# Row normalisations of a two-layer attention and expert kernel computed inside the output stages

## The reference

```
x = x + xattn0(LN(x), ctx, mask)              # 16 heads of 16, then @ Wo.T
s = LN(x)
s1 = LN(s + selfattn(s) @ Wo + bo) * ln1_g + ln1_b
expert = floor(s1 @ router_w + router_b) mod 4    # top-1 expert of each row
x = x + (LN(s1 + expert_ffn(s1)) * ln2_g + ln2_b)
x = x + xattn1(LN(x), ctx, side bias) @ Wo.T + bo
z = LN(x)                                     # top-2 of 16 experts, capacity 320
x = x + experts(z) + mean of 2 shared experts(z)
```

## Time and profile before

| | |
|---|---|
| time, median of 3 runs | 1940.11 us (1938.03 to 1944.42) |
| profiled execution | 1940.5 us |
| its span, first to last instruction | 1938.7 us |
| TensorE busy | 1603.3 us, 83% |
| VectorE busy | 1117.1 us, 58% |
| ScalarE busy | 789.6 us, 41% |
| GpSimd busy | 466.5 us, 24% |

### The profile page before, as it was taken

One profiled execution on the slowest core, in us unless ns is written; L12 is line 12 of the kernel. 1 busy time (PEld: TensorE's weight loads), 2 busy tenths in 40 slices (PEclk: granted clock), 3 DMA queues, 4 the chain that ended last, 5 costly groups with the idle time before them and its releaser, 6 DMA issues. The chain is left out here.

```text
span 1938.7 us, 24242 instructions
## 1 busy us (share of the span) xinstructions
PE 1603.3 (83%) x8256; PEld 1036.7 (53%) x8256; DVE 1117.1 (58%) x2686; ACT 789.6 (41%) x1239; POOL 466.5 (24%) x245
## 2 busy tenths in 40 slices
PE   6799999888999994199717389899868999899993
PEld 3466666554444433199714256556554556566672
DVE  6699999475576747222287488888663441122224
ACT  2388888321455561022103477777612122111110
POOL 0000000020000001311100699999522134111111
PEclk9799999996799997599959699999978999899997
DMA  7533332033222204455335798887342001644424
GB/s 265 199 96 99 98 99 77 24 143 99 55 67 67 77 23 147 160 177 196 122 115 225 256 313 296 284 297 277 133 192 70 1 25 63 209 140 152 153 70 143
DMA packets 136800, 276.56 MB, mean 143 GB/s; under 512 B 23792, under 2 KB 65904, under 8 KB 127088
## 3 DMA queue, kind: packets, MB, share of 16 engines
q1 hardware_dynamic: 129312, 258.98, 40.1%
q0 software_dynamic: 5264, 14.06, 2.1%
q10 hardware_dynamic: 2112, 2.10, 0.3%
HBM read 215.36 MB, written 59.69 MB: 142 GB/s over the span
## 5 line engine op out<-in xcount | busy, mean ns | idle before, releaser
L667 DVE CUSTOM_DVE_ANT_0 X<-pS,M 128x512 f32<-128x512 f32 x512 | 340.2, 689 | 77.2 <-POOL M L593 50.5
L607 PE MATMUL pS<-k,q 65*128 65x512 f32 (+1 forms) x512 | 255.5, 502 | 84.4 <-DVE mx L667 50.1
L593 POOL TENSOR_TENSOR M<-C,M 128x2048 f32<-128x2048 f32 x64 | 290.5, 4588 | 132.5 <-DMA M<-in_fside_Bx16xSxS 132.4
L616 PE MATMUL pT<-ident,X 128*128 128x128 f32 x2048 | 308.3, 274 | 0.3 <-ACT PT L703 0.3
L616 PEld LDWEIGHTS pT<-ident,X 128*128 128x128 f32 x2048 | 256.1, 141 | 40.4 <-issue 3.8
L848 DVE TENSOR_REDUCE nm<-pS 128x1 fp32r<-128x512 f32 x256 | 167.9, 687 | 86.3 <-PE pS L790 74.7
L607 PEld LDWEIGHTS pS<-k,q 65*128 65x128 f32 (+1 forms) x512 | 98.7, 193 | 209.1 <-DVE mx L667 122.5
L500 PE MATMUL pO<-PT,V 128*17 128x512 f32 x1536 | 207.1, 615 | 1.0 <-ACT OT L875 1.0
L695 ACT ACTIVATE X<-X,nm 128x512 f32<-128x512 f32 x256 | 164.0, 712 | 34.6 <-DVE nm L673 34.6
L695 ACT ACTIVATE X<-X,mx 128x512 f32<-128x512 f32 x256 | 164.7, 715 | 21.0 <-DVE mx L667 21.0
L680 DVE COPY PT<-pT 128x1024 f32<-128x1024 f32 x128 | 156.1, 1220 | 6.4 <-PE pT L616 6.4
(11 more groups left out here) (263 smaller groups left out, 2155.8 us busy)
## 6 DMA issues: line engine op xcount, KB each, us to landing
M<-in_fside_Bx16xSxS SPq DMA_DIRECT2D x64, 1024.0 KB, 7.1
w<-in_L_ffn_ew SPq DMA_DIRECT2D x48, 512.0 KB, 4.3
w<-in_L_ffn_W SPq DMA_DIRECT2D x23, 1024.0 KB, 5.4
q<-q_stacks SPq DMA_DIRECT2D x192, 64.0 KB, 3.1
k<-k_stacks SPq DMA_DIRECT2D x128, 64.0 KB, 2.9
M<-mask SPq DMA_DIRECT2D x16, 512.0 KB, 3.6
xs<-top_in SPq DMA_DIRECT2D x51, 128.5 KB, 5.0
k_stacks<-hi SPq DMA_DIRECT2D x24, 256.0 KB, 2.1
```

What stands on the lines that cost most here:

```text
L593: eng.tensor_tensor(M[:, slot], C[:, b % 2], M[:, slot], ALU.subtract).then_inc(s_m, 1)
L607: eng.matmul(pS[:, qt % 2, :], of, by, start=True, stop=True).then_inc(s_s, 1)
L616: ins = eng.transpose(pT[:, kt, qt * P:(qt + 1) * P], X[:, t % 3, qt, kt * P:(kt + 1) * P], self.ident[:])
L667: eng.tensor_tensor_reduce(X[:, i % 3, qt, :], pS[:, qt % 2, :], M[:, slot, qt, :], 2.0 if mask is None else 1.0, HIGHEST if mask is None ...
```

## The change

The normalisations of projection 1, of `route_top1` and of `route_and_share` are taken out of these stages and done by VectorE and ScalarE in the output stage ahead, batch by batch: statistics of a row tile right behind its add, variance and square root per batch, and the scaling of a batch behind the second add of the next. The normalised rows are written over the rows of O that TensorE has already transposed (tile Z, or xx for the router). The weights wo, bo, the projection weights of projection 1 and ln1's rows are fetched in the middle of the attention ahead; those of projections 0 and 2 stay where they were. The normalisations in projections 0 and 2 and in `combine_top1` stay.

```diff
-        self.zeros = self.sb("zeros", [P, S])
+        self.zeros = self.sb("zeros", [P, D])
+        self.Z = self.sb("Z", [P, NT, D + 1])
...
-    def norm_and_transpose(self, block, ctx, bank, banks, src, nat, featT, before=None):
-
-
-        s_ch, s_mv, s_rs, s_z, s_tr, s_ev = (self.sem(n, ctx) for n in ("s_ch", "s_mv", "s_rs", "s_z", "s_tr", "s_ev"))
-        rs = self.normalise(block, s_ch, s_mv, s_rs, s_z, nat, src, ctx, before=before)
+    def turn_rows(self, block, ctx, bank, banks, src, nat, featT, before=None, normal=False):
+
+
+        s_tr, s_ev = (self.sem(n, ctx) for n in ("s_tr", "s_ev"))
+        if not normal:
+            s_ch, s_mv, s_rs, s_z = (self.sem(n, ctx) for n in ("s_ch", "s_mv", "s_rs", "s_z"))
+            rs = self.normalise(block, s_ch, s_mv, s_rs, s_z, nat, src, ctx, before=before)
+
+            @block.scalar
+            def _(eng):
+                self.deviations(eng, s_mv, s_rs, rs)
 
         def tensor(eng, tenant_gone=None):
             for b in range(B):
-                eng.wait_ge(s_z, b + 1)
+                if not normal:
+                    eng.wait_ge(s_z, b + 1)
...
+    def load_weights(self, eng, wq, wk, wv, bq, bk, bv):
+
+        self.s_w = self.sem("s_w")
+        for w, of in zip(self.W, (wq, wk, wv)):
+            eng.dma_start(w[:], of.rearrange("(k p) n -> p k n", p=P)).then_inc(self.s_w, 16)
+        if bq is not None:
+            eng.dma_start(self.bias[:, 0, :], bq).then_inc(self.s_w, 16)
+            eng.dma_start(self.bias[:, 1, :], bk).then_inc(self.s_w, 16)
+            eng.dma_start(self.bvr[:], bv.partition_broadcast(P)).then_inc(self.s_w, 16)
+
+    def load_out(self, eng, wo, bo):
+
+        self.s_wo = self.sem("s_wo")
+        eng.dma_start(self.wo[:], wo.rearrange("(k p) n -> p k n", p=P)).then_inc(self.s_wo, 16)
+        if bo is not None:
+            eng.dma_start(self.bo[:], bo.partition_broadcast(P)).then_inc(self.s_wo, 16)
+
+
+    def project(self, src, nat, qT, kvT, context, q_scale, QS, KS, biased=True, fetch=None, normal=False, mask=None, common=None, first=False, ring=None):
...
-                    for w, of in zip(W, (wq, wk, wv)):
-                        eng.dma_start(w[:], of.rearrange("(k p) n -> p k n", p=P)).then_inc(s_w, 16)
-                    if n_bias:
-                        eng.dma_start(bias[:, 0, :], bq).then_inc(s_w, 16)
-                        eng.dma_start(bias[:, 1, :], bk).then_inc(s_w, 16)
-                        eng.dma_start(bvr[:], bv.partition_broadcast(P)).then_inc(s_w, 16)
+                    if fetch is not None:
+                        fetch(eng)
...
                     for i in range(NBH):
+                        if i == NBH // 2:
+                            fetch(eng)
...
                     for pair in range(NBH // 2):
+                        if pair == NBH // 4:
+                            fetch(eng)
...
-                @block.sync
-                def _(eng):
-                    eng.dma_start(w[:], wo.rearrange("(k p) n -> p k n", p=P)).then_inc(s_w, 16)
-                    if bo is not None:
-                        eng.dma_start(brow[:], bo.partition_broadcast(P)).then_inc(s_w, 16)
...
                 def _(eng):
-                    for n in range(B * KD):
-                        b, k = divmod(n, KD)
-                        eng.wait_ge(s_tr, n + 1)
-                        need(eng, s_y, (b - 1) * ST)
-                        eng.copy(OT[:, b % 2, k, :], bank[:, n % 4, :]).then_inc(s_ev, 1)
+                    def deviations(b):
+                        eng.wait_ge(s_var, b + 1)
+                        rows = slice(b * ST, (b + 1) * ST)
+                        eng.activation(rs[:, rows], rs[:, rows], ACT.Sqrt).then_inc(s_dev, 1)
+
+                    for b in range(B):
+                        for k in range(KD):
+                            n = b * KD + k
+                            eng.wait_ge(s_tr, n + 1)
+                            need(eng, s_y, (b - 1) * ST)
+                            eng.copy(OT[:, b % 2, k, :], bank[:, n % 4, :]).then_inc(s_ev, 1)
+                        if b >= 2:
+                            deviations(b - 2)
+                    deviations(B - 2)
+                    deviations(B - 1)
 
                 @block.vector
                 def _(eng):
-                    if bo is not None:
-                        eng.wait_ge(s_w, 32)
+                    if biased:
+                        eng.wait_ge(self.s_wo, 32)
                         for b in range(B):
                             rows = slice(b * ST, (b + 1) * ST)
                             eng.tensor_tensor(dst[:, rows, :], base[:, rows, :], brow[:].unsqueeze(1).to_broadcast([P, ST, D]),
                                               ALU.add).then_inc(s_b, 1)
-                        eng.wait_ge(s_b, B)
-                    src = base if bo is None else dst
-                    for n in range(NT):
-                        eng.wait_ge(s_y, n + 1)
-                        eng.tensor_tensor(dst[:, n, :], src[:, n, :], py[:, n % 4, 0:D], ALU.add).then_inc(s_a, 1)
-
-
-    def route_top1(self, src, xx, gain, shift, slot, tile_expert, XS):
+                    src = dst if biased else base
+
+                    def stats(n):
+                        eng.wait_ge(s_a, n + 1)
+                        eng.bn_stats(st[:, n, :], dst[:, n, :]).then_inc(s_st, 1)
+
+                    def scale(b):
+                        rows = range(b * ST, (b + 1) * ST)
+                        eng.wait_ge(s_dev, b + 1)
+                        eng.reciprocal(rs[:, b * ST:(b + 1) * ST], rs[:, b * ST:(b + 1) * ST]).then_inc(s_rs, 1)
+                        eng.wait_ge(s_rs, b + 1)
+                        eng.wait_ge(s_tr, (b + 1) * KD)
+                        if affine is None:
+                            for n in rows:
+                                eng.tensor_scalar(z[:, n, :], dst[:, n, :], mv[:, n, 0:1], rs[:, n:n + 1], ALU.subtract, ALU.mult)
+                            return
+                        gain, shift, s_affine = affine
+                        if b == 0:
+                            eng.wait_ge(s_affine, 32)
+                        for n in rows:
+                            eng.scalar_tensor_tensor(out=z[:, n, :], in0=dst[:, n, :], scalar=mv[:, n, 0:1], in1=gain[:],
+                                                     op0=ALU.subtract, op1=ALU.mult).then_inc(s_g, 1)
+                        for n in rows:
+                            eng.wait_ge(s_g, n + 1)
+                            eng.scalar_tensor_tensor(out=z[:, n, :], in0=z[:, n, :], scalar=rs[:, n:n + 1], in1=shift[:],
+                                                     op0=ALU.mult, op1=ALU.add)
+
+                    for b in range(B):
+                        for j in range(ST):
+                            n = b * ST + j
+                            if biased and j == 0:
+                                eng.wait_ge(s_b, b + 1)
+                            eng.wait_ge(s_y, n + 1)
+                            eng.tensor_tensor(dst[:, n, :], src[:, n, :], py[:, n % 4, 0:D], ALU.add).then_inc(s_a, 1)
+                            if j > 0:
+                                stats(n - 1)
+                            if j == 1 and b > 0:
+                                scale(b - 1)
+                        stats((b + 1) * ST - 1)
+                        eng.wait_ge(s_st, (b + 1) * ST)
+                        for n in range(b * ST, (b + 1) * ST):
+                            eng.bn_aggr(mv[:, n, :], st[:, n, :]).then_inc(s_ag, 1)
+                        eng.wait_ge(s_ag, (b + 1) * ST)
+                        eng.tensor_scalar(rs[:, b * ST:(b + 1) * ST], mv[:, b * ST:(b + 1) * ST, 1], EPS, None, ALU.add).then_inc(s_var, 1)
+                    scale(B - 1)
...
-                rs = self.normalise(block, s_ch, s_mv, s_rs, s_z, xx[:, :, 0:D], src, ctx, gain=grow, shift=brow,
-                                    ready=lambda eng: eng.wait_ge(s_w, 64))
-
-                @block.scalar
-                def _(eng):
-                    self.deviations(eng, s_mv, s_rs, rs)
...
-                    eng.wait_ge(s_z, B)
+                    eng.wait_ge(s_w, 32)
...
-                turn_rows, take_rows, s_zT = self.norm_and_transpose(block, ctx, pt, 2, src, z[:, :, 0:D], zT)
+                turn_rows, take_rows, s_zT = self.turn_rows(block, ctx, pt, 2, src, z[:, :, 0:D], zT, normal=True)
...
+            def fetch(eng):
+                p.load_out(eng, t["L0_xattn_Wo"], None)
+                p.load_weights(eng, f["Wq"], f["Wk"], f["Wv"], f["bq"], f["bk"], f["bv"])
+            p.attention_turned(QS, KS, Z, fetch, mask=mask)
+            p.output(Z, False, p.x, p.x, Z)
...
+                    p.project(p.x, Z, sT, sT, None, -DK ** -0.5, QS, KS, normal=True, ring=ring)
+                s_affine = p.sem("s_affine")
+
+                def fetch(eng):
+                    p.load_out(eng, f["Wo"], f["bo"])
```

(56 more changed lines are left out.)

53 lines of the change are left out of this document (24 added, 29 removed).

## The result

The changed kernel takes 1910.75 us (median of 4 runs, 1909.51 to 1912.70), the kernel before 1942.07 in the same comparison (4 runs, 1938.03 to 1944.42). The ratio is 0.984, with an interval of 0.982 to 0.986: faster by 31 us. The profiled execution has a span of 1909.2 us against 1938.7.

A forecast was written before the change was run, and what follows sets the result against it. No engine was full: at three output stages TensorE paced, then stood while VectorE normalised. Gains 3.3 + 7.5 + 14.4 = 25.2 us warm, 20.8 cold, less 2; 21.5 taken: 1940.5 - 21.5 = 1919 us, range 1912 to 1929.

The forecast's parts named there:

- VectorE ends the outputs: Output stages: VectorE, not TensorE, ends them, at 5.0 us a batch, or 7.1 with gain and shift.
- the landing of rw: Router's block after the second output: the second small transfer lands 4.6 us after the block's start, as before.
- Place A: First output and second projection, first transpose to first projection matmul: 37.7 us becomes 34.4, gain 3.3.
- Place B: Second output and router, up to the first router dot product: 45.8 us becomes 38.3, gain 7.5.
- Place C: Third output and top-2 router, up to the gate matmul: 47.1 us becomes 32.7, gain 14.4, about 8.4 from the memset collision.
- Cold or warm start: TensorE's clock at the start of Places B and C: a low one costs 2.2 us each; sum 25.2 warm, 20.8 cold.
- Fetches -1: Attentions: early weight fetches issued in front of q and k loads cost 0 to 3 us, taken as 1 over all three.
- Cover behind B -1: Router's scatter to first xs load: W2 in front of W1 and xs costs 0 to 5 us or more, taken as 1.
- Rival 1: Output stages: VectorE finishes each instruction before the next, 1935 us (chance 0.06), or 1944 with an extra wait each (0.02).
- Rival 2: Behind Place B: W2 and W1 make the tiles start as late as before, 1926 us; chance 0.12 with partial forms.
- Rival 3: After the outputs: TensorE, made to wait, stays at 1.2 GHz for a projection, 1950 us; chance 0.02.
- a gain above my sum: Whole kernel: the gain exceeds the sum of the forecast's terms; chance 0.03.

The follow-up runs named there:

- the scalings on ScalarE: Changed kernel with the scalings of the first and third output moved from VectorE to ScalarE: 1901.6 us, ratio 0.981.
- the second profile: The changed kernel, unaltered, run again in the same rounds as the kernel before: 1908.8 us, ratio 0.984.
- The memset alone: Kernel before with one line making GpSimd's memset of the top-2 blank wait until the rows are turned: 1934.7 us, ratio 0.996.
- either half: Changed kernel with only its early fetches, 1927.0 us, or with only its normalisations moved into the output stages, 1925.6 us; ratio 0.992 each.
- both improvements: Changed kernel with the router's rb and rw fetched in the second attention and first and third output scalings on ScalarE: 1900.2 us, ratio 0.979.
- the three old profiles: Kernel before, profiled first (1942.07 us) and again (1940.9 us), and kernel before with GpSimd's top-2 memset delayed (1934.7 us).

## Why the prediction was wrong in size, step by step

The mechanism held: VectorE ends the outputs, and all three places got shorter. What failed are the sizes of the terms for A, B and C, each put too small by 1.6 to 2.7 us: the first add at A, the cost of a batch, and the landing of rw.

- **VectorE ends the outputs; a middle batch costs 5.0 and 7.1 us.** Right, and shown by the scalings on ScalarE. Mis-sized: 4.76 and 6.63. The reciprocal of 4 columns takes 0.16 us, not the 0.25 of 16, the batch's variance overlaps the next add (378.48 and 378.55), and a group of four scalings lets the next instruction start 0.08 us before its own end (379.75 + 1.38 and 381.05), twice in B. For three batches that is 0.7 us at A and C and 1.4 at B.
- **Place A, gain 3.3.** It was 5.9, and 4.6 in the second profile (33.1 us). The failing step is the first add "5.4 us after the start": I took away the wait of 1.1 and kept the rest of a start at half clock. It is 2.96 at full and 4.5 at half clock. With it the chain took 24.4 us from the start to the transposes instead of 27.9; the transposes, at a clock of 0.60 where it was 0.75 before, gave 0.9 back (7.4 instead of 6.5).
- **Place B, gain 7.5.** It was 10.2. Up to the block's end 31.8 us instead of 33.7, most of it the smaller batches, and rw landed 3.7 us into the block instead of 4.6. That this fetch was still on the path was right: without it B is 31.9.
- **Place C, gain 14.4, of it 8.4 the memset.** It was 16.0, or 13.7 in the second profile. The transposes started 24.4 us into the place instead of 25.4, most of it the smaller batches, and the gate came 6.7 us behind them instead of 7.3. The memset alone gave 7.1 at its place and 7.9 in the median.
- **Cold or warm start.** The 21.5, between 23.2 and 18.8, mixed two cases; both occur (31.1 and 33.4 for the same C). The low clock was put at 2.2 us a place; it cost 2.3 at this C and 1.5 at B (37.1 against 35.6 for the same code).
- **Fetches -1.** About -2 in attention 2, nothing to be seen in attention 0 (281.1 us before, 281.2 on average over the eight profiles with the change). The forecast's own sign of being wrong, an attention over 2 us longer, did come in the first profile (323.6 against 320.4). **Cover behind B -1.** Right: 1.1 (28.05 against 26.91 us from the first scatter to the first xs load).
- **Rival 1 (VectorE one at a time, 1935 to 1944).** Out: 0.33 us. Its mechanism exists in one form, an instruction waiting for the one just ahead, at 0.12 us each.
- **Rival 2 (B given back).** Out: 28.05 us from scatter to xs where 32 would have shown it.
- **Rival 3 (TensorE stays at 1.2 GHz for a projection).** Out: 57.1 us for it, less than before. But the clock did decide several us, in a stage that I didn't look at.
- **Not foreseen.** The shared expert is 2 us longer on average with the change (212.9 over eight profiles against 210.9 and 210.8), 216.8 with either half, and 214.8 with the memset's line alone. Part of it is the clock at its start: over its first 15 us 0.66 in both profiles of the kernel before and in the shortest stage of all (210.4, both improvements), 0.60 in the changed kernel, 0.54 to 0.55 in six others (212.9 to 216.8). At these three levels ScalarE comes out of the same wait of 10.3 us at 58.2, 59.8 and 61.5 us into the stage. And in five of 14 profiles ScalarE stood still late in the stage, here in the changed kernel:
```profile
1590.85 0.37 ACT L1670 COPY common<-py 128x256 f32<-128x256 f32 x1 [2.44 <-PE py L1637]
1599.37 0.65 ACT L1670 COPY common<-py 128x256 f32<-128x256 f32 x2 [8.15 <-remote]
```
The same waits in the kernel before are 3.08 us, and TensorE lost 2.1 us by it. The five are this profile and all four that were taken on one chip; none of the eight taken on three other chips has it, so it may go with the chip and not with an edit. What it is stays open.

The forecast's error is thus mostly in its own terms: 25.2 us for the three places with a warm start, 32.1 measured in the one profile and 28.6 in the other, and 2 us taken off for effects that cost 3. That leaves 26 to 29 us of the 31.3 and 32.4 in the medians. The rest is of the size of what changed in projection 1 and attention 1, 1.2 and 6.9 us shorter on average than in the three old profiles, less what the shared expert gives back; the forecast had no term for them, and whether the change causes them stays open. That the total fell 1.25 us outside the range, and not inside, is within the swing of some 5 us; that the gain is half as large again as the sum is not. The range had 0.03 for "a gain above my sum", though three of its terms were rounded the same way.

## What to carry to other kernels

Price a stage at both levels of TensorE's clock and keep both cases, not their mean; and before a difference of a few us is put down to an edit, compare the granted clock of the stages that the edit doesn't touch, and at the start of those that it does. Take a big instruction of GpSimd out from beside VectorE's work first: a line that delays it was worth 7.9 us here, where the whole change was worth 31. Work laid into another engine's stage is free only until the engine that takes it ends the stage; a third engine with gaps (ScalarE here) can take the part that overflows. Let a VectorE instruction need the result of the last but one, not of the last.

## What was not expected of the hardware

- The same attention takes 261 to 275 us by its mean granted clock of 0.93 to 0.87.
- A VectorE instruction that waits for the one just ahead starts 0.45 us after it, an independent one 0.33.
- ScalarE scales and shifts 128x256 elements in 0.52 us (four in 2.07) where VectorE takes 0.35 (four in 1.38), and changed its table once an output, in 1.28 us, for square roots, copies and scalings together.
